# Stores of the first feed-forward product three tiles behind their sums, the loads of the down weights one to two tiles later, and batch 1's routing one tile later

## The reference

```
logits = einsum('bsh,he->bse', x, gate_w);  routing_weights = top_k(logits, 2)
h          = relu(einsum('bsh,hi->bsi', x, up_w)) ** 2          # 1024 -> 2048
shared_out = einsum('bsi,ih->bsh', h, down_w)                   # 2048 -> 1024
x_latent   = einsum('bsh,hl->bsl', x, fc1_w)                    # 1024 -> 512
routed_out = (x_latent @ expert_w) * sum(routing_weights) @ fc2_w
out        = layernorm(shared_out + routed_out, ln_gamma, ln_beta)
```

## Time and profile before

| what | us |
|---|---|
| median of 3 runs (lowest, highest) | 674.84 (672.65, 676.1) |
| profiled execution: its own time | 673.77 |
| profiled execution: span from first to last instruction | 672.0 |
| PE busy in the span | 608.9 (91%) |
| DVE / ACT / POOL busy | 408.4 / 307.3 / 142.4 |
| first product, first to last matmul | 229.1 to 463.5 |

### The profile page before, as it was taken

The page is one execution under the profiler, slowest core; times in us unless marked ns, Lnnn a source line. Parts: engine busy times, 40 slices in busy tenths (PEclk is TensorE's granted clock), DMA queues, the critical chain, the costliest instruction groups (busy, mean ns, idle before and its releaser), DMA issues.

```text
span 672.0 us, 7903 instructions
## 1 busy us (share of the span) xinstructions
PE 608.9 (91%) x2951; PEld 490.8 (73%) x2960; DVE 408.4 (61%) x538; ACT 307.3 (46%) x400; POOL 142.4 (21%) x178
## 2 busy tenths in 40 slices
PE   2886998998798899899899999998999999999992
PEld 2675887775476488588688888886888888888881
DVE  4856799999977235433432333234875556649876
ACT  4565567869767242433332433103343433323625
POOL 2534265757542023242200000000000000002100
PEclk9989899999999799999999999999999999999997
DMA  9773555537573785968978946401333335179913
GB/s 341 277 226 92 158 147 147 175 101 192 175 232 110 254 276 205 323 232 303 314 277 281 304 170 218 157 1 32 125 94 95 94 95 173 78 250 304 265 58 125
DMA packets 86326, 125.61 MB, mean 187 GB/s; under 512 B 23952, under 2 KB 54928, under 8 KB 86288
## 3 DMA queue, kind: packets, MB, share of 16 engines
q1 hardware_dynamic: 78816, 97.31, 44.8%
q0 software_dynamic: 5168, 19.40, 8.9%
q10 hardware_dynamic: 2304, 8.39, 3.8%
HBM read 85.23 MB, written 35.65 MB: 180 GB/s over the span
## 4 chain that ended last, share of the span: by engine, by line
PE 57%; DVE 5%; DMA 2%; ACT 1%; issue 1%; SPq 0%; DVEq 0%
PE acc_b L1527 28%; PE acc_a L1559 15%; PE acc_b L1559 12%; DMA u_raw<-in_L_ffn_up_w_dram 2%; PE acc_a L1493 1%; PE acc_a L1494 1%; PE acc_a L1481 1%; DVE d_raw L1781 1%; ACT u_hi L1602 0%; DVE stat_n L1876 0%; DVE ffn_lo L1895 0%; DVE ffn_hi L1895 0%; DVE ffn_hi L1884 0%; DVE ffn_lo L1884 0%; DVE u_lo L1749 0%
## 5 line engine op out<-in xcount | busy, mean ns | idle before, releaser
L1749 DVE TENSOR_TENSOR u_lo<-u_raw,u_hi 128x1024 fp32r<-128x1024 f32 x18 | 23.8, 1325 | 108.4 <-ACT u_hi L1602 108.4
L1527 PE MATMUL acc_b<-x2T_hi,u_hi 128*128 128x512 f32 x160 | 63.3, 396 | 3.2 <-DVE u_lo L1749 3.2
L1527 PE MATMUL acc_b<-x2T_hi,u_lo 128*128 128x512 f32 x160 | 62.4, 390 | 0.0
L1527 PE MATMUL acc_b<-x1T_hi,u_hi 128*128 128x512 f32 x160 | 62.3, 390 | 0.0
L2020 POOL DMA_DIRECT2D x1T_hi<-r_scratch x4 | 2.9, 712 | 280.6 <-PE acc_a L1559 272.6
L1527 PE MATMUL acc_b<-x2T_lo,u_hi 128*128 128x512 f32 x160 | 62.3, 389 | 0.0
L1527 PE MATMUL acc_b<-x1T_hi,u_lo 128*128 128x512 f32 x160 | 62.3, 389 | 0.0
L1527 PE MATMUL acc_b<-x1T_lo,u_hi 128*128 128x512 f32 x160 | 62.2, 389 | 0.0
L337 PE MATMUL qkv_ps<-w_hi,xT_hi 128*128 128x512 f32 (+1 forms) x128 | 37.2, 374 | 16.4 <-POOL w_lo L1105 8.3
L1602 ACT ACTIVATE u_hi<-u_raw 128x1024 fp32r<-128x1024 f32 x18 | 19.0, 1056 | 56.2 <-DMA u_raw<-in_L_ffn_up_w_dram 33.1
L1559 PE MATMUL acc_a<-x1T_hi,x2T_hi 128*128 128x512 f32 x168 | 39.1, 389 | 0.0
(11 more groups left out here) (263 smaller groups left out, 1407.6 us busy)
## 6 DMA issues: line engine op xcount, KB each, us to landing
d_raw<-in_L_ffn_down_w_dram SPq DMA_DIRECT2D x20, 512.0 KB, 6.0
t_scratch<-d_raw SPq DMA_DIRECT2D x20, 512.0 KB, 4.4
d_raw<-t_scratch SPq DMA_DIRECT2D x20, 512.0 KB, 3.8
c_sb<-in_ctx_dram ACTq DMA_DIRECT2D x16, 512.0 KB, 3.9
u_raw<-in_L_ffn_up_w_dram SPq DMA_DIRECT2D x16, 512.0 KB, 7.5
r_scratch<-f1b SPq DMA_DIRECT2D x10, 512.0 KB, 3.2
r_scratch<-f2b SPq DMA_DIRECT2D x10, 512.0 KB, 3.1
x_sb<-in_x_dram SPq DMA_DIRECT2D x8, 512.0 KB, 5.0
```

The lines of the kernel that those rows point to most:

```text
L1527: mm = pe.matmul(acc_b[:, q % 4], s, v, start=(k == 0 and i == 0), stop=(k == KT - 1 and i == 2))
L1749: dve.tensor_tensor(u_lo[:, m % 2], u_raw[:, m % 2], u_hi[:, m % 2].bitcast(F32), ALU.subtract).then_inc(S["u_lo_done"], 1)
```

## The change

SP's loop now runs two tiles further. `load_u(m)` comes first in every turn, as before. The stores of round k move from the turn of `load_b(k + 1)` (or, for the last round, the turn behind it) to turn `sums_at(k) + 3`: 5, 6, 8, 9, 10, 12, 13, 14, 16, 17. The loads of rounds 0 and 1 stay in turns 2 and 3; those of rounds 2 to 9 move two turns down, to 7, 8, 9, 11, 12, 13, 15, 16. In a turn with both, the stores now come ahead of the load. `routing(1)` moves from behind tile 3 to behind tile 4 on PE, `transpose_logits(1)` from 4 to 5, `spread_r(1)` from 6 to 7, and ACT's and DVE's parts go along by one tile.

```diff
@@ sync
-            for m in range(2, MU):
-                load_u(m)
+            for m in range(2, MU + 2):
+                if m < MU:
+                    load_u(m)
                 for k in range(NP):
-                    if m == sums_at(k):
+                    if m == sums_at(k) + 3:
+                        store_stage(k)
+                        store_t(k)
+                for k in range(NP):
+                    if m == sums_at(k) + (0 if k < 2 else 2):
                         load_b(k)
-                        if k:
-                            store_stage(k - 1)
-                            store_t(k - 1)
-                if m == sums_at(NP - 1) + 1:
-                    store_stage(NP - 1)
-                    store_t(NP - 1)
@@ tensor
-                if m == 3:
+                if m == 4:
                     routing(1)
-                if m == 4:
+                if m == 5:
                     transpose_logits(1)
-                if m == 6:
+                if m == 7:
                     spread_r(1)
@@ scalar
                 if m == 3:
                     spread_out(0)
+                if m == 4:
                     logits_out(1)
-                if m == 7:
+                if m == 8:
                     spread_out(1)
@@ vector
-                if m == 5:
+                if m == 6:
                     route(1)
```

## The result

| | median us | lowest to highest | runs |
|---|---|---|---|
| before | 672.67 | 670.70 to 676.52 | 8 |
| changed | 667.64 | 664.54 to 668.86 | 8 |

The ratio is 0.9916, with a 95% interval of 0.9892 to 0.9940: the changed kernel is faster by 5.7 us of 672.67 (4.0 to 7.3); the two medians lie 5.03 us apart. The profiled execution of it took 668.24 us, its span is 666.5 us. The forecast was 669.0 us, 5.84 us less than the 674.84 us that three runs of before had given; over eight runs before is at 672.67, from which the same sum would have given 666.8.

A forecast was written before the change was run, and what follows sets the result against it. PE was taken to bound the kernel, with two waits in the first product to remove: -2.62 - 3.22 = -5.84 us, from the median of 674.84 to 669.0 us. The range for 8 in 10 was 666.0 to 672.3 us.

The forecast's parts named there:

- the two gaps: PE's two waits inside the first product: 2.62 us ahead of batch 1's routing, 3.22 us ahead of tile 8.
- Part 1: First product: routing one tile later puts tile 4's matmuls over the ACT copy it waits for; -2.62 us.
- gap A: PE's wait ahead of batch 1's routing, for ACT's copy after tile 3; 2.62 us, forecast to go whole.
- Part 2: First product, SP's order: u loads no longer behind the stores of the round before; -3.22 us.
- gap B: PE's wait ahead of tile 8 for `u_lo`, its u load issued late behind stores; 3.22 us, forecast to go.
- The cover: First product, u loads: 19.0 us to land against at most 9.4 us needed, leaving 9.6 us of room.
- Rival 2: First product: down_w loads bound it if landings average above 10.6 us; 683.8 us; 3% about 674, 4% slower.
- Rival 3: Second product's start: the slow clock behind the 3.3 us gap, costing 1.86 us, may not occur; 667.1 us, 11%.

The follow-up runs named there:

- the last two: DVE's first split of the second product made early, added to the changed kernel (ratio 0.9838) and to SP's old order with the routing behind tile 7 (0.9836).

## Why the prediction was right, and which step was not

**The bound and the sum.** PE bounds the first product, and the two gaps are what went. The sum of 5.84 us stands against 6.30 us in the profiles' stretch and 5.7 us in the ratio. The second product started at 461.28, forecast 461.0, though the first began 0.8 us later than before.

**Part 1, the routing (2.62 us).** The gap went as argued, the ACT copy lying under tile 4. But the routing alone is worth 4.86 us of the stretch. The step that failed is that gap A's 2.62 us are all that the move brings: I looked at who waits for the routing, not at which loop the routing's own 3.70 us now stand in parallel to. The chain of before could have told: its path to tile 8 begins at the end of tile 4, and the routing moved from ahead of that point to behind it.

**Part 2, SP's order (3.22 us).** Alone it does give that (3.47 in the stretch). On top of part 1 it gives 1.44 us: 217.48 less 216.04. The two terms were right one by one and wrong as an attribution; that the sum came out rests on gap B being removed completely and only once. That both parts share a gap was in no rival, so the sum's coming out owes something to luck. The mechanism, u loads held behind stores that wait for the sums, is shown by the kernel with SP's order alone, whose wait for `u_lo` is gone, and by the one with stores at + 1, where it comes back.

**The cover.** u loads land in 9.2 us at most, with 19 us of room, as said. The new waits of ACT and DVE for `d_raw` came in the rounds that were forecast (3, 4, 6, 7 and 9, 1.9 to 5.9 us each on ACT), and cost nothing, as the kernel with the loads one turn earlier shows.

**Rival 2's threshold** was set somewhat too high. Its round was p = L + 5.9 us, L being the landing. In the changed kernel rounds 3 and 4 start 14.26 us apart (ACT's L1626 at 309.57 and 323.83) with 7.6 us to land the loads between them, rounds 6 and 7 12.79 us apart (353.37 and 366.16) with 6.5 us. So the fixed part is 6.3 to 6.7 us; the term that was too small is the issue of the loads, 2.2 to 2.6 us for the two against 0.81 before. Out of the 16.5 us that a round may take, it leaves a mean landing of 9.8 to 10.2 us, not 10.6, an estimate from these two pairs of rounds. The changed kernel's median of 7.2 stayed under it. The price was also too small per us of wait: in the kernel with loads three turns down a wait of 3.93 us cost 7.0.

**Rival 3, the clock at the second product's start,** neither came nor went in the two profiles: 29.06 us before and 29.05 after for that phase. Two of the other kernels' profiles did not have it, so it may differ from one execution to the next. What the prediction said there of gaps A and B goes too far in one point: the row of the Trainium skill (TensorE: Matmul & The Clock Gate, section on why this matters for your kernels) speaks of gaps longer than A's 2.62 us, so by it only gap B would have cost clock; the clock was 1.00 behind both the earlier trace rows.

## What to carry to other kernels

When two edits each take away a wait, look whether the waits lie on one loop: work moved from ahead of the loop's start to behind it is slack for everything that the loop ends in, and the gains don't add. In a queue that runs in order, as SP's does here, a load should stand where what is ahead of it has long been ready; how far ahead matters only until the wait is covered (here two turns did as well as three, one, with the loads of down_w earlier too, cost the whole gain). When an experiment moves work out of a loop, measure the loop again, since it may have become shorter for another reason than the one under test. And a gap of the bounding engine is worth more than its length if the clock falls behind it.

## What the runs showed of the hardware

**The clock behind a gap.** The gap of 3.1 us between the products, the same in every kernel but the last two, was followed by a stretch at half clock in seven profiles (that phase took 28.92 to 29.08 us instead of 27.20) and by none in two, which took 27.45 us: the routing alone, and the stores at + 1. The window of the first of these over that place:

```profile
460.00:470.00 10.00, 8.83 (x39) 7.37 (x40) 9.93 (x9) 3.03 (x4) 0.00 (x0) 1.00 0.43 121
```

Inside the first product, gap B (3.22 us) kept 2.4 GHz, 3.93 us was followed by a mean of 0.57 and 4.65 us by 0.79 over 340 to 348 us. So 3.93 us of wait cost 7.0 us and 4.65 us of it 6.5 (121.58 us instead of 119.7). The Trainium skill (TensorE: Matmul & The Clock Gate, section on why this matters for your kernels) asks for no long idle gaps between bursts of matmuls. The rows behind 3.93 and 4.65 us agree; those behind gap B and behind two of nine gaps of 3.1 us don't, so a gap of about that length may or may not cost.

**The issue of a DMA is not of fixed length on SP.** A u load takes 0.38 us to issue in the changed kernel (median 379 ns) and 1.01 us before. The other kernels sort the same way by the stores: 0.38 to 0.46 us in the five that have the stores three turns behind the sums, 1.00 to 1.10 in the six with stores at + 1 or + 2. The median landing of the u loads sorts with it: 4.7 to 5.7 us against 6.7 to 7.3. What makes an issue long is not shown: before, the u load at 305.21 went out right behind stores and took 0.48 us. A load of down_w takes 0.43 us to issue before and 1.20 us after, behind the stores. Its landing does not sort by the stores: it is 7.8 us with the stores at + 2 and at + 1, where the load stands ahead of them in a turn, and 7.2 in the changed kernel.
